# A composite convolution as three half-length products by column parity, with its folds moved forward

## The reference, cut to what matters

```python
x = x + ffn0(cond0(x, cond_512, ...), A, B, Wr)                # level 0: 64 adapters of rank 16, top 16 by router score
x = x + ffn1(cond1(x, cond_512, ...), qweight, scales, zeros, bias)  # level 1: int4 weights, 1024 x 1024

# cond, for layer i, typ in enumerate(('same', 'upsample', 'same', 'downsample')):
s = style @ mw.T + mb
weight = SCALE * w * s[:, None, :, None]
weight = weight * rsqrt(sum(weight * weight, axis=(2, 3)) + EPS)[:, :, None, None]
# 'same': 3 taps; 'upsample': transposed conv with stride 2, then a 4-tap blur;
# 'downsample': the blur, then a conv with stride 2
```

## Time and profile before

| | |
|---|---|
| median of 3 runs | 992.88 us (990.76 to 996.49) |
| time of the profiled execution | 990.33 us |
| its span, first to last instruction | 988.8 us |
| PE (TensorE) busy | 940.2 us, 95% of the span |
| DVE busy | 558.3 us, 56% |
| ACT (ScalarE) busy | 376.2 us, 38% |
| POOL busy | 111.0 us, 11% |
| mean granted clock of TensorE | 0.978 of full |

### The profile page before, as it was taken

One profiled execution on the slowest core, in us unless ns is written; L12 is line 12 of the kernel. 1 busy time (PEld: TensorE's weight loads), 2 busy tenths in 40 slices (PEclk: granted clock), 3 DMA queues, 4 the chain that ended last, 5 costly groups with the idle time before them and its releaser, 6 DMA issues.

```text
span 988.8 us, 14065 instructions
## 1 busy us (share of the span) xinstructions
PE 940.2 (95%) x4636; PEld 792.4 (80%) x4636; DVE 558.3 (56%) x1133; ACT 376.2 (38%) x717; POOL 111.0 (11%) x141
## 2 busy tenths in 40 slices
PE   5899999999999999999999998839999999999997
PEld 4777888888888888888888887638888888888886
DVE  8894353353353354344344333966677767777774
ACT  2672243243243243233233221434554445444541
POOL 7100000000000000000000000710112111211121
PEclk8799999999999999999999999859999999999999
DMA  8701011011011011101101101331221222112211
GB/s 281 244 5 65 22 42 64 21 42 64 21 42 64 25 39 64 40 25 63 42 28 57 42 21 54 54 106 29 100 85 64 65 96 94 64 64 87 96 50 64
DMA packets 33567, 64.12 MB, mean 65 GB/s; under 512 B 12304, under 2 KB 13968, under 8 KB 33552
## 3 DMA queue, kind: packets, MB, share of 16 engines
q1 hardware_dynamic: 24480, 30.90, 10.6%
q0 software_dynamic: 9072, 33.03, 9.2%
HBM read 47.14 MB, written 16.78 MB: 65 GB/s over the span
## 4 chain that ended last, share of the span: by engine, by line
PE 88%; DVE 8%; issue 2%; ACT 1%; DMA 1%; POOL 0%; SPq 0%; POOLq 0%; DVEq 0%; ACTq 0%
PE conv_ps L172 9%; PE conv_ps L174 8%; PE conv_ps L173 8%; PE fold_ps L581 6%; PE prod_ps L743 6%; PE prod_ps L744 6%; PE prod_ps L745 6%; PE prod_ps L725 6%; PE prod_ps L726 6%; PE prod_ps L727 6%; PE prod_ps L824 6%; PE prod_ps L823 6%; PE fold_ps L548 3%; PE turn_ps L682 3%; PE turn_ps L704 1%
## 5 line engine op out<-in xcount | busy, mean ns | idle before, releaser
L158 DVE TENSOR_TENSOR h_lo<-conv_ps,h_hi 64x512 fp32r<-64x512 f32 x128 | 88.2, 689 | 47.3 <-ACT h_hi L637 46.4
L172 PE MATMUL conv_ps<-h_hi,e_hi 128*128 128x512 f32 x256 | 104.9, 410 | 2.4 <-issue 2.4
L657 ACT ACTIVATE cond<-conv_ps,bias,demod_tab 128x510 f32<-128x510 f32 x64 | 49.9, 779 | 144.7 <-PE conv_ps L174 132.7
L173 PE MATMUL conv_ps<-h_lo,e_hi 128*128 128x512 f32 x256 | 102.2, 399 | 0.0
L174 PE MATMUL conv_ps<-h_hi,e_lo 128*128 128x512 f32 x256 | 102.1, 399 | 0.0
L743 PE MATMUL prod_ps<-b_hi,xt 128*128 128x512 f32 x256 | 99.9, 390 | 2.3 <-DVE xt L158 2.3
L823 PE MATMUL prod_ps<-quant,xt_hi 128*128 128x512 f32 x256 | 100.3, 392 | 1.4 <-DVE xt_lo L158 1.4
L801 DVE SCALAR_TENSOR_TENSOR res<-prod_ps,norm,res 128x512 f32<-128x512 f32 x32 | 23.9, 750 | 137.3 <-PE prod_ps L745 137.3
L726 PE MATMUL prod_ps<-a_lo,xt 128*128 128x512 f32 x256 | 101.0, 395 | 0.0
L725 PE MATMUL prod_ps<-a_hi,xt 128*128 128x512 f32 x256 | 101.0, 394 | 0.0
L727 PE MATMUL prod_ps<-a_hi,xt 128*128 128x512 f32 x256 | 101.0, 394 | 0.0
(11 more groups left out here) (222 smaller groups left out, 1982.4 us busy)
## 6 DMA issues: line engine op xcount, KB each, us to landing
x_in<-in_x SPq DMA_DIRECT2D x64, 128.0 KB, 2.7
res<-in_x POOLq DMA_DIRECT2D x16, 512.0 KB, 3.6
x_after_first<-res POOLq DMA_DIRECT2D x16, 512.0 KB, 2.9
x_in<-x_after_first SPq DMA_DIRECT2D x64, 128.0 KB, 2.7
res<-x_after_first POOLq DMA_DIRECT2D x16, 512.0 KB, 3.5
out_x<-res POOLq DMA_DIRECT2D x15, 512.0 KB, 2.9
a_raw<-in_adapter_in SPq DMA_DIRECT2D x8, 512.0 KB, 8.1
b_raw<-in_adapter_out SPq DMA_DIRECT2D x8, 512.0 KB, 8.0
```

What stands on the lines that cost most here:

```text
L158: return nc.vector.tensor_tensor(out, whole, hi.bitcast(F32), ALU.subtract)
L172: nc.tensor.matmul(out, hi(w), moving_hi(i), start=(i == 0), stop=False)
L173: nc.tensor.matmul(out, hi(w), moving_lo(i), start=False, stop=False)
```

## The change

The composite convolution of a sample reads and writes columns in pairs. After the change it is done by the parity of the columns. With even and odd columns of `h` apart (256 each), three products of half length with two filters each take the place of one of full length with four: a middle product of summed filters with the even columns (`CENTRE`), and two products with the differences of odd and even columns (`BEFORE`, `AFTER`). That is 18 matmuls of 256 columns for a sample. The sums of filters and the differences of columns are made on POOL, from unsplit float32 values in SBUF (`whole`, `data`, in one scratch buffer that both samples share), and split into hi and lo after that. The output is put together by DVE (`dve_join`). The output pairs are shifted by one position, so the layouts of `cond`, of the adapter and router rows and of the int4 rows are rolled. `x_raw` lies in the memory of `x_lo`, so its load waits for the product that reads `x_lo`. Rows of x in DRAM are padded to 514 columns for each phase.

```diff
+        def pool_taps(pool, c, bufs):
+            pool.wait_ge(S.fold2_whole, c + 1)
+            nc.gpsimd.tensor_tensor(flat(bufs.whole[:, 4:6, :, :]), flat(bufs.whole[:, 0:4:2, :, :]), flat(bufs.whole[:, 1:4:2, :, :]), ALU.add).then_inc(S.taps_summed, 1)
...
         def act_fold2(act, c, bufs, first=False):
             act.wait_ge(S.fold2_done, c + 1)
+            act.wait_ge(S.layer1_ready, 2 * c + 2)
...
+            nc.scalar.activation(flat(whole[:, 0:E_PAIRS, :, 0:C]), blocks, ACT.Identity)
+            nc.scalar.activation(flat(whole[C:P, 0:E_PAIRS, :, C:P]), blocks[0:C, :, :], ACT.Identity)
+            nc.scalar.activation(flat(whole[0:C, 0:E_PAIRS - 1, :, C:P]), blocks[C:P, 2:2 * E_PAIRS, :], ACT.Identity)
+            nc.scalar.activation(whole[0:C, E_PAIRS - 1, :, C:P], zero_block[0:C, :, :], ACT.Identity).then_inc(S.fold2_whole, 1)
...
+        def act_taps(act, c, bufs, first=False):
+            act.wait_ge(S.taps_summed, c + 1)
...
+            nc.scalar.activation(flat(bufs.e_hi[:, :, :, :]), flat(bufs.whole), ACT.Identity).then_inc(S.fold2_hi, 1)
...
+        def dve_taps(v, c, bufs):
+            v.wait_ge(S.fold2_hi, c + 1)
+            low(flat(bufs.e_lo[:, :, :, :]), flat(bufs.whole), flat(bufs.e_hi[:, :, :, :])).then_inc(S.fold2_ready, 1)
...
-        def act_layer1(act, c, a, bufs):
+        def act_layer1(act, c, a, bufs, first=False):
             act.wait_ge(S.layer1_done, 2 * c + a + 1)
+            if a == 1 or not first or bufs.first_sample:
+                act.wait_ge(S.layer1_ready, 2 * c + a)
...
+            nc.scalar.activation(even, by_parity[:, 0, :], ACT.Identity, bias=..., scale=...)
+            nc.scalar.activation(odd, by_parity[:, 1, :], ACT.Identity, bias=..., scale=...).then_inc(S.layer1_scaled, 1)
+        def pool_differences(pool, c, a, bufs):
+            pool.wait_ge(S.layer1_scaled, 2 * c + a + 1)
+            centre = bufs.data[:, CENTRE:CENTRE + SPAN]       # SPAN = 257
+            nc.gpsimd.tensor_tensor(bufs.data[:, BEFORE:BEFORE + SPAN], bufs.data[:, ODD:ODD + SPAN], centre, ALU.subtract)
+            nc.gpsimd.tensor_tensor(bufs.data[:, AFTER:AFTER + SPAN], bufs.data[:, ODD + 1:ODD + 1 + SPAN], centre, ALU.subtract).then_inc(S.differences, 1)
+        def act_layer1_hi(act, c, a, bufs):
+            act.wait_ge(S.differences, 2 * c + a + 1)
+            nc.scalar.activation(bufs.h_hi[a][:, :], bufs.data[:, 0:3 * SPAN], ACT.Identity).then_inc(S.layer1_hi, 1)
         def dve_layer1(v, c, a, bufs):
             v.wait_ge(S.layer1_hi, 2 * c + a + 1)
-            low(bufs.h_lo[a][0:C, 1:H + 1], conv_ps[a][0:C, :], bufs.h_hi[a][0:C, 1:H + 1])
-            low(bufs.h_lo[a][C:P, 2:H + 2], conv_ps[a][C:P, :], bufs.h_hi[a][C:P, 2:H + 2]).then_inc(S.layer1_ready, 1)
+            low(bufs.h_lo[a][:, :], bufs.data[:, 0:3 * SPAN], bufs.h_hi[a][:, :]).then_inc(S.layer1_ready, 1)
...
-            products(conv_ps[a][:, :], (3, 2, 1, 0), ...).then_inc(S.cond_done, 1)
+            part(fold_ps[a][:, 0:T2], (5, 4), CENTRE).then_inc(S.middle_done, 1)     # T2 = 256
+            part(conv_ps[a][:, 0:T2], (3, 1), BEFORE)
+            part(conv_ps[a][:, T2:H], (2, 0), AFTER).then_inc(S.cond_done, 1)
...
+        def dve_join(v, c, a, bufs):
+            v.wait_ge(S.cond_done, 2 * c + a + 1)
+            v.wait_ge(S.middle_scaled, 2 * c + a + 1)            # from act_middle, which scales fold_ps[a]
+            nc.vector.scalar_tensor_tensor(out=out, in0=both, scalar=..., in1=middle, op0=ALU.mult, op1=ALU.add).then_inc(S.joined, 1)
+        def act_ends(act, c, a, bufs):
+            act.wait_ge(S.joined, 2 * c + a + 1)
...
+            nc.scalar.activation(bufs.cond[C:P, a, 0:H:H - 1], ends[C:P, :], ACT.Identity).then_inc(S.cond_ready, 1)
...
             with pool.Fori(0, NPAIR - 1) as i:
+                conv_pool(i + 1, buf0)                 # differences (0), differences (1), taps
                 pool.wait_ge(S.x1_ready, 2 * i + 3)
-                pool.dma_start(x_scratch[i], buf0.res[:, :]).then_inc(S.x1_stored, 16)
+                pool.dma_start(x_scratch[i][:, :, 0:H], phases(buf0.res)).then_inc(S.x1_stored, 16)
...
             with pool.Fori(0, NPAIR - 1) as i:
+                pool_differences(pool, i + NPAIR + 1, 0, buf1)
+                pool_differences(pool, i + NPAIR + 1, 1, buf1)
                 add_bias(i + NPAIR)
+                pool_taps(pool, i + NPAIR + 1, buf1)
                 pool.wait_ge(S.y_ready, i + 1)
...
+            for a in range(2):
+                pe_cond(pe, NPAIR, a, buf1)            # level 1's first pair, now ahead of the edge products
...
             with pe.Fori(NPAIR, 2 * NPAIR - 1) as i:
                 c = i + 1
+                pe_fold3(pe, c, buf1)
                 pe_layer1(pe, c, 0, buf1)
...
                 pe_layer1(pe, c, 1, buf1)
-                pe_fold3(pe, c, buf1)
+                pe_fold2(pe, c, buf1)
                 pe_quant(pe, i, 0, buf1)
-                pe_fold2(pe, c, buf1)
                 pe_quant(pe, i, 1, buf1)
...
@@ scalar, first_step
                 act_fold3(act, c, buf0)
+                act_layer1_hi(act, c, 0, buf0)
                 act_layer1(act, c, 1, buf0)
                 act_scores(act, i, buf0)
+                act_layer1_hi(act, c, 1, buf0)
...
@@ vector, first_step
                 dve_gated_turn(v, i, buf0)
+                v.wait_ge(S.gated_turned, 2 * i + 2)
+                for a in range(2):
+                    dve_join(v, c, a, buf0)
...
@@ vector, second_step
-                dve_fold_start(v, c, buf1)
+                dve_fold3(v, c, buf1)
                 dve_turn(v, i, buf1)
                 dve_layer1(v, c, 0, buf1)
-                dve_fold3(v, c, buf1)
+                dve_reduce(v, i, buf1)
                 dve_layer1(v, c, 1, buf1)
-                dve_reduce(v, i, buf1)
-                dve_fold2(v, c, buf1)
+                dve_taps(v, c, buf1)
                 if not last:
+                    dve_fold_start(v, c + 1, buf1)
                     split(c + 1, buf1)
                 dve_rowsum(v, i, buf1)
                 dve_second_residual(v, i, buf1)
+                for a in range(2):
+                    dve_join(v, c, a, buf1)
```

282 lines of the change are left out of this document (168 added, 114 removed).

## The result

The changed kernel takes 1192.32 us (median of four runs, 1188.56 to 1192.71) against 992.8 before: the ratio is 1.200, with a 95% interval of 1.195 to 1.204. The prediction said 1146 us, 1108 to 1188. The direction and most of the mechanism are as forecast; the time lies 46 us above the forecast and 4 above the range.

The account below looks back on a forecast made before the run. It took PE, busy 95%, as the bound before the change. Level 1's 120, level 0's 12, the start's 10 and the stage between's 12.5 sum to 154.5 on 990.33, 1144.8; it predicted 1146 us, range 1108 to 1188.

Parts of the forecast that it names:

- one serial cycle through POOL, ACT, DVE and PE: Level 1: a step takes 28.2 us against 18.6 of PE's list, so PE waits; +120 us over the level.
- the holding by the bias: Level 1: DVE's lo of sample 1 waits for POOL's add_bias, which puts 1.57 us in the step.
- PE's saving: Cond as 18 matmuls at 0.118 us takes 2.12 us, not 2.79: 0.67 a sample, 43 us for 64 samples.
- POOL's store is issued at 308.05: Level 0: with level 1's store-to-load time and issue, POOL is free for the differences 5.77 us after layer 1 starts.
- POOL's DMAs cost more: Rival: rows of 2 KB double the pieces; twice the 0.53 us issue adds 24 us, 1170 us; chance 0.12.
- SP's wait on layer 1: The wait before the shifted load of x lies more than 10 us ahead of the split and costs nothing.
- level 0's PE waits once, at full clock: Level 0: PE waits 2.2 us before cond and saves 1.34: +0.9 a step, +12 us over 14 steps.
- The rival of the falling clock: Level 1: PE's idle gap brings 1.2 GHz, PE comes 2.5 us late a step, 38 us, 1184 us; chance 0.14.
- the ends of the levels: First pair's start adds 10 us (3 to 15), the stage between the levels 12.5 (5 to 18).
- PE as the bound: Rival: all of the new chain hides and PE's saving stands, 947 us in the loops, some 955 with the start; chance 0.04.
- the shorter chain: Rival: DVE isn't held by the bias (24 us less) or hand-overs cost nothing, 1108 to 1125 us; chance 0.14.
- the slow 256-column product: Rival: 256-column products take 0.15 us, level 0 loses 20 us and level 1 nothing, 1166 us; chance 0.02.

Follow-up runs that it names:

- e6: Changed kernel with, in level 1, a data buffer for each sample and whole and middle in places of their own: 1132.39 us, ratio 1.140.
- e3: Changed kernel without GpSimd's addition of the bias in level 1, so the output lacks the bias: 1171.74 us, ratio 1.181.
- e4: Kernel before the change, with cond alone as 18 matmuls of 256 columns a sample in place of 12 of 512: 957.73 us, ratio 0.966.
- e2: Changed kernel with level 0's residual store, its wait and the next load of res on SP's queue in place of POOL's: 1144.61 us, ratio 1.151.
- e12: Changed kernel with ACT's copy of the scores ahead of the scaling of sample 1 in level 0: 1214.1 us, ratio 1.224.
- e9: e8 with one wait more: SP issues level 0's loads of x only after the first half of the hidden product: 1163.58 us, ratio 1.173.
- e1: Changed kernel with the stored rows of x_after_first at a stride of 528 words in place of 514: 1176.46 us, ratio 1.187.
- e8: Changed kernel with x_after_first in rows of 1024 words without pads; DVE writes the two pad words: 1180.78 us, ratio 1.191.
- e5: Changed kernel with level 1's split and fold start of the next pair ahead of e_lo on DVE, ACT's fold start before e_hi: 1175.26 us, ratio 1.184.
- e13: e11 without GpSimd's addition of the bias in level 1, so the output lacks the bias: 987.05 us, ratio 0.994.
- e11: Changed kernel with DMAs moved to SP, separate buffers and reordered lists, plus edge layers 0 and 1 ahead of the conds between levels: 1003.16 us, ratio 1.009.

## Why the prediction was right, and where it was wrong

**Right.** PE stops being the bound, and level 1 becomes one serial cycle through POOL, ACT, DVE and PE: +114.8 us for +120. Its parts hold one by one, within 0.3 us each. POOL begins the differences 909.82 - 904.80 = 5.0 us behind `y_ready` in e6 and 929.31 - 924.28 = 5.0 in the changed kernel, where 4.84 was set; the holding by the bias is 1.3 us (e3 takes it out, 1.23 a step) where 1.57 was set; the shared buffer, which the sum has in it as a wait and not as a term of its own, costs 3.6 us a step (e6). The Trainium skill's page SBUF — State Buffer (section Who interferes with whom) says that the second to issue of such a pair waits for the whole of the first; the trace agrees: the bias ends at 907.34 + 2.40 = 909.74, and lo (1), issued at 908.30, at 910.55, 0.81 behind that, where its own time is 0.96. PE's saving is 34.7 us (e4) for 43: the 18 matmuls take 2.26 us (e2), not 2.12, and the first pairs of the levels save nothing. This had no weight here, as PE wasn't the bound. A small slip in the prediction's last sum: 1144.8 and the 2.5 us by which the median lies higher give 1147.3, and it put 1146.

**Wrong: the step "POOL's store is issued at 308.05 and, with level 1's 3.60 to the load and 0.53 for it, POOL is free at +5.77".** It took the old landing for the new store. The store takes 5.2 us in place of 2.9 (5.4 and 5.5 in e3, e6 and e12, which leave it as it is) and its issue 0.68. Level 0 lies 38.8 us above its forecast, and the steps at full clock say how much of that is the landing. They take 40.1 us in the changed kernel and 37.7 in e9, where the landing is back at 2.9 and PE's wait at the score sum is gone: 14 x 2.4, an estimate of 34 us. The clock adds about 2.5, as above. The last 2 to 3 are mostly the 0.3 us by which a step of e9 still exceeds 37.4; they weren't followed up. (By the totals, 562.3 us for the 14 steps and 531.6 in e9, it would be 30.7, but e9 has three steps with matmuls at half clock, two early ones of 39.6 and 39.3 us and the last, which cost it 5.5.) The chain behind POOL was right: with the old landing PE waits 1.95 us before cond in e9, where 2.2 was forecast. Two sentences of the prediction had the causes in hand. The padded rows were in it as a rival, but only as twice the time of an issue ("POOL's DMAs cost more", 24 us, 0.12); the issue grew by 0.15 and the landing by 1.7. And SP's wait on layer 1 was costed at nothing, since it lies "more than 10 us ahead of their split"; true for the split, but the wait moved 512 KB of loads onto POOL's store, 0.6 us of landing.

**Wrong: level 0's PE waits once, at full clock.** It waits twice. The wait at the score sum isn't on the chain (e12: without it no time is won), but waits lower the clock. The rival of the falling clock was priced for level 1 alone, and there it happened at no cost: 20 of the 36 matmuls of the cond at 917.32 are at half clock, and from step to step it is between some 12 and 27 of them while the step stays at 27.8 us, since `y_ready` comes later still. In level 0 it has a price, but in the changed kernel a small one: about 2.5 us in all, 1.1 of them in the one step shown above. With the first wait gone and the second at 2.3 it cost e1 and e8 some 10 us each, and with 3.7 us in one piece it cost e12 1.8 us a step.

**Mis-sized: the ends of the levels.** Start and first step cost 16.9 for 10, the stage between the levels 17.6 for 12.5, where the bounds were 3 to 15 and 5 to 18. Part of that is the one execution: e1, e3, e5 and e12 have 13.5 to 19.0 and 13.5 to 15.5. Between the levels fold 2 begins 45.1 us behind turn 15 here, 41.0 to 43.3 in those runs and 40.7 in the kernel before. The tables' loads, now issued behind the last hidden product, are one candidate, for which the sum had only POOL's 2 us; no run tests it, and the cause stays open. How the start's 7 us divide was only read from traces: PE waits 6.4 us for `e_lo` before the first cond.

**The rivals.** PE as the bound, the shorter chain, POOL's issue and the slow 256-column product don't come true. The range ended at 1188 because each mishap was taken by itself, as the prediction says of it. The DMAs had 24 us as a rival and cost an estimated 34, by the landing and not by the issue, and the ends of the levels came some 12 above their terms on top of that; level 1, 5 us under its forecast, took a little of it back.

**Can the saving be had?** Not by this kernel's means. With the chain broken up, PE is the bound in both levels only when the bias is left out (e13, 0.994). With it the best is 1.009 (e11): against the kernel before, level 0 gains 0.9 us a step and level 1 nothing, and the longer start and the longer stage between the levels cost 18.6 and 8 us. Splitting the bias away from DVE's two-input instructions, by a second `res` buffer, wasn't tried.
